# Layer 0's linear attention as two phases in one loop: a hybrid transformer on one Trainium2 core

## The reference, cut to what matters

```python
q  = x + x @ Wq.T + bq
ks = x + einsum(x, Wk) + bk        # two sets
vs = x + einsum(x, Wv) + bv        # two sets
q, ks = silu(q) + 0.5, silu(ks) + 0.5
q  = q / (norm(q) + 1e-6);  ks = ks / (norm(ks) + 1e-6)       # by head of 8 channels
states = einsum('kbhnd,kbhne->kbhde', ks * scale, vs * scale)
state  = prod(states, axis=0)      # the product of the two sets
out = q @ state                    # by head
out = (out - mean) * rsqrt(var + 1e-5) * ln_g + ln_b
out = out @ Wo.T + bo
```

## Time and profile before

| | |
|---|---|
| median of three runs | 6225.26 us (6223.73 to 6227.15) |
| the profiled execution's own time | 6223.72 us |
| its span, first to last instruction | 6221.8 us |
| PE busy in the span | 3906.2 us, 63% |
| DVE busy | 3758.3 us, 60% |
| ACT busy | 2448.4 us, 39% |
| POOL busy | 1708.2 us, 27% |
| mean granted TensorE clock | 0.795 of full speed |

### The profile page before, as it was taken

The page is one execution under the profiler, slowest core; times in us unless marked ns, Lnnn a source line. Parts: engine busy times, 40 slices in busy tenths (PEclk is TensorE's granted clock), DMA queues, the critical chain, the costliest instruction groups (busy, mean ns, idle before and its releaser), DMA issues. The chain is left out here.

```text
span 6221.8 us, 78605 instructions
## 1 busy us (share of the span) xinstructions
PE 3906.2 (63%) x21844; PEld 2459.3 (40%) x21844; DVE 3758.3 (60%) x6990; ACT 2448.4 (39%) x4474; POOL 1708.2 (27%) x1709
## 2 busy tenths in 40 slices
PE   5756648466664488724666664688855847476474
PEld 3546438222233233322222223344434636454464
DVE  4323651599974677544888886655567635566354
ACT  2334226355532277613545443233333524243242
POOL 0043014355542355422333340000001140301412
PEclk8868659688876699856778785799966779887898
DMA  2012003100001222012000000000000011100111
GB/s 82 0 55 75 1 10 91 41 1 0 0 4 54 74 82 89 22 36 79 0 1 0 0 0 2 18 1 0 0 2 2 2 45 41 39 8 2 45 42 51
DMA packets 224866, 170.50 MB, mean 27 GB/s; under 512 B 27435, under 2 KB 211602, under 8 KB 223714
## 3 DMA queue, kind: packets, MB, share of 16 engines
q1 hardware_dynamic: 204130, 125.44, 6.8%
q0 software_dynamic: 20480, 41.98, 2.3%
HBM read 92.02 MB, written 74.45 MB: 27 GB/s over the span
## 5 line engine op out<-in xcount | busy, mean ns | idle before, releaser
L1775 POOL TENSOR_TENSOR XN<-s_l_attn_a_h,LOG 128x512 f32<-128x512 f32 x512 | 642.5, 1276 | 768.6 <-DVE s_l_attn_a_h L1815 753.5
L1815 DVE TENSOR_TENSOR_SCAN s_l_attn_a_h<-s_l_attn_a_da,XN 128x512 f32<-128x512 f32 x512 | 598.5, 1211 | 142.9 <-ACT s_l_attn_a_da L1760 102.7
L1751 PE MATMUL s_l_attn_a_y_ps<-XN,c_ident 128*128 128x512 f32 x1024 | 588.7, 704 | 25.2 <-DVE s_l_attn_a_y L2027 15.4
L1760 ACT ACTIVATE s_l_attn_a_da<-s_l_attn_a_delta,s_l_attn_a_a 128x510 f32<-128x510 f32 x512 | 353.3, 690 | 526.0 <-DVE s_l_attn_a_h L1815 525.5
L483 DVE COPY s_l_ffn_ffn_xt<-s_l_ffn_ffn_turned 128x128 f32<-128x128 f32 x416 | 120.9, 292 | 711.1 <-PE s_l_ffn_ffn_turned L604 709.5
L569 POOL DMA_INDIRECT s_l_ffn_ffn_back<-slots_y,s_l_ffn_ffn_slots x320 | 302.8, 946 | 875.3 <-DMA slots_y<-PICK 566.4
L623 PE MATMUL s_l_ffn_ffn_down<-down,s_l_ffn_ffn_hid 128*128 x2944 | 421.1, 284 | 193.4 <-DVE s_l_ffn_ffn_hid L496 186.0
L623 PEld LDWEIGHTS s_l_ffn_ffn_down<-down,s_l_ffn_ffn_hid 128*128 128x128 f32 x2944 | 361.2, 192 | 233.6 <-issue 228.5
L416 ACT COPY s_l_ffn_ffn_own_w<-up 128x512 f32 (+2 forms) x416 | 305.0, 734 | 375.4 <-DVE s_l_ffn_ffn_expert_no L467 277.3
L1730 PE MATMUL s_l_attn_a_spread<-s_l_attn_a_parts,s_l_attn_a_pick 96*128 96x512 bf16 x512 | 182.2, 443 | 390.3 <-DVE XN L1806 243.2
L561 POOL DMA_INDIRECT slots_x<-XN,s_l_ffn_ffn_slots x320 | 311.5, 973 | 388.9 <-DVE s_l_ffn_ffn_slots L460 293.2
(11 more groups left out here) (631 smaller groups left out, 8651.3 us busy)
## 6 DMA issues: line engine op xcount, KB each, us to landing
XNT<-slots_x SPq DMA_DIRECT2D x32, 640.0 KB, 6.3
slots_y<-LOG SPq DMA_DIRECT2D x16, 640.0 KB, 4.3
slots_y<-PICK SPq DMA_DIRECT2D x16, 640.0 KB, 4.3
s_l_attn_b_qr<-s_l_attn_b_q_rows SPq DMA_DIRECT2D x64, 144.0 KB
s_l_attn_b_kr<-s_l_attn_b_k_rows SPq DMA_DIRECT2D x64, 144.0 KB
XNT<-slots_x SPq DMA_DIRECT2D x8, 768.0 KB, 7.0
slots_x<-PICK SPq DMA_DIRECT2D x10, 512.0 KB, 6.4
slots_x<-XN,s_l_ffn_ffn_slots POOLq DMA_INDIRECT x320, 2.2
```

What stands on the lines that cost most here:

```text
L1751: last = self.nc.tensor.matmul(self.y_ps[:, i, :], self.k.ident[:], self.hc[n % 2][:, i, :], start=(n == 0), stop=(n == NST - 1))
L1760: self.nc.scalar.activation(self.da[:, i, :, 1:], self.delta[par][:, i, :].rearrange("p (b t) -> p b t", b=BPG)[:, :, 1:], ACT.Exp, scale= ...
L1775: self.nc.gpsimd.tensor_tensor(self.hc[n % 2][:, i, :], self.h[n % 2][:, i, :], self.c_rows[n % 2], ALU.mult).then_inc(self.hc_ready, 1)
L1815: self.nc.vector.tensor_tensor_scan(self.h[n % 2][:, i, :], self.da[:, i, :, :].rearrange("p b t -> p (b t)"), self.u[n % 2][:, i, :], 0.0 ...
```

## The change

The steps of a pair are split into two phases. Phase A is everything from the copy of `xg` to the masked state; phase B is everything from the product with the state to the addition to `k.X`. A helper `over_phases` runs phase A of the first pair alone, then a loop of 7 rounds, each with phase A of the next pair and phase B of this pair mixed together, and then phase B of the last pair alone. The order within a round is written out by hand for each engine. The two batches of a pair now share one `proj` and one `proj_v`: PE's projection of a batch waits until DVE has read the one before it (`since(pe, biased, u)`). The transposed queries go into banks of `proj`, the states have a bank of their own for each `m`, and the output's projection goes into `o_ps`. The output's bias matmul now stands behind the wait for `ont_ready`. `take_stats` is removed, and `build` sets `k.stats_taken` to false behind `l0_attn_b`.

The diff, cut to its core:

```diff
-        proj = s.two_ps("proj", [P, TPB, 4 * D])
-        mid, late = s.ps("mid", [P, 2, 2, SEQ]), s.ps("late", [P, 2, 2, SEQ])
...
+        proj, proj_v = s.ps("proj", [P, TPB, 4 * D]), s.ps("proj_v", [P, TPB, 2 * D])
+        st, late = s.two_ps("st", [P, 512]), s.two_ps("late", [P, 512])
+        turned_q_ps = [proj[:, m, 0:SEQ] for m in range(2)]
+        st_ps = [b[:, 0:2 * D].rearrange("p (i d) -> p i d", i=2) for b in st]
+        o_ps = [b[:, 0:SEQ].rearrange("p (t d) -> p t d", d=D) for b in late]
+        turned_o_ps = [b[:, SEQ:2 * SEQ] for b in late]
...
+        def over_phases(engine, step):
+
+            step(0, None)
+            with engine.Fori(0, PAIRS - 1) as pair:
+                step(pair * 2 + 2, pair * 2)
+            step(None, BATCH - 2)
...
 # TensorE
+            def project(u, m):
+                pe.wait_ge(xg_ready, u + 1)
+                since(pe, biased, u)
+                for t in range(TPB):
+                    xt = xg[m][:, t * P:(t + 1) * P]
+                    nc.tensor.matmul(proj[:, t, :], xt, w["L0b_w"][:, 0:4 * D], start=True, stop=True)
+                    last = nc.tensor.matmul(proj_v[:, t, 0:D], xt, w["L0b_w"][:, 4 * D:5 * D], start=True, stop=True)
+                last.then_inc(projected, 1)
+
+            def take_from_state(u, m):
+                pe.wait_ge(done, u + 1)
+                pe.wait_ge(state_ready, u + 1)
+                pe.wait_ge(qt_ready, u + 1)
...
+            def project_out(u, m):
+                pe.wait_ge(ont_ready, u + 1)
+                nc.tensor.matmul(o_ps[m], k.ones_row[0:1, 0:P], w["L0b_bo"][:], start=True, stop=False, skip_group_check=True)
...
+            def step(a, b):
+                if a is not None:
+                    project(a, 0)
+                if b is not None:
+                    take_from_state(b, 0)
+                    take_from_state(b + 1, 1)
+                if a is not None:
+                    project(a + 1, 1)
+                if b is not None:
+                    turn_out(b, 0)
+                    turn_out(b + 1, 1)
+                    project_out(b, 0)
+                    project_out(b + 1, 1)
+                if a is not None:
+                    turn_and_add_up(a, 0)
+                    turn_and_add_up(a + 1, 1)
...
 # ScalarE
+            def step(a, b):
+                if a is not None:
+                    keep_x(a, 0)
+                    keep_x(a + 1, 1)
+                    activate(a, 0)
+                    activate(a + 1, 1)
+                if b is not None:
+                    keep_out(b, 0)
+                    keep_out(b + 1, 1)
+                if a is not None:
+                    roots(a, 0)
+                    roots(a + 1, 1)
+                    keep_qt(a, 0)
+                    keep_qt(a + 1, 1)
...
 # VectorE
+            def step(a, b):
+                if a is not None:
+                    add_bias(a, 0)
+                if b is not None:
+                    variance(b, 0)
+                    variance(b + 1, 1)
+                if a is not None:
+                    add_bias(a + 1, 1)
+                if b is not None:
+                    normalise(b, 0)
+                    normalise(b + 1, 1)
+                if a is not None:
+                    square(a, 0)
+                    square(a + 1, 1)
+                    scale(a, 0)
+                    scale(a + 1, 1)
+                if b is not None:
+                    add_out(b, 0)
+                    add_out(b + 1, 1)
+                if a is not None:
+                    mask_state(a, 0)
+                    mask_state(a + 1, 1)
...
-                take_stats(nc, dve, k, pair * (2 * TPB), 2 * TPB)
...
-            k.stats_taken = step not in ("l3_attn_a", "l2_ffn", "l3_attn_b", "l1_attn_a", "l1_attn_b", "l2_attn_a")
+            k.stats_taken = step not in ("l0_attn_b", "l3_attn_a", "l2_ffn", "l3_attn_b", "l1_attn_a", "l1_attn_b", "l2_attn_a")
```

More of the change, by code:

```diff
@@ L1006, in l0_attn_b @@
     HD = 8
-    BPG = 1
+    PAIRS = BATCH // 2
     with Scope(nc, name) as s:
@@ L1045, in _ @@
         def _(pe):
-            pe.wait_ge(w_ready, 1)
[L1047 to L1089, removed]
@@ new lines, in project @@
+            def project(u, m):
[10 more added lines that the diff above has]
+                pe.wait_ge(qt_ready, u + 1)
+                for t in range(TPB):
+                    last = nc.tensor.matmul(o_ps[m][:, t, :], qt[m][:, t * P:(t + 1) * P], state[m][:], start=True, stop=True)
+                last.then_inc(o_ready, 1)
@@ new lines, in turn_out @@
+            def turn_out(u, m):
+                pe.wait_ge(on_ready, u + 1)
+                for t in range(TPB):
+                    last = nc.tensor.transpose(turned_o_ps[m][:, t * P:(t + 1) * P], on[m][:, t, :], k.ident[:])
+                last.then_inc(turned_o, 1)
+            def project_out(u, m):
+                pe.wait_ge(ont_ready, u + 1)
+                nc.tensor.matmul(o_ps[m], k.ones_row[0:1, 0:P], w["L0b_bo"][:], start=True, stop=False, skip_group_check=True)
+                for t in range(TPB):
+                    last = nc.tensor.matmul(o_ps[m][:, t, :], ont[m][:, t * P:(t + 1) * P], w["L0b_wo"][:], start=False, stop=True,
+                                            skip_group_check=True)
+                last.then_inc(y_ready, 1)
@@ new lines, in turn_and_add_up @@
+            def turn_and_add_up(u, m):
+                pe.wait_ge(unit, u + 1)
+                for t in range(TPB):
+                    last = nc.tensor.transpose(turned_q_ps[m][:, t * P:(t + 1) * P], a[m][:, t, 0:D], k.ident[:])
+                last.then_inc(turned_q, 1)
+                for i in range(2):
+                    for t in range(TPB):
+                        last = nc.tensor.matmul(st_ps[m][:, i, :], a[m][:, t, (1 + i) * D:(2 + i) * D], z[m][:, t, (3 + i) * D:(4 + i) * D],
+                                                start=(t == 0), stop=(t == TPB - 1))
+                last.then_inc(stated, 1)
@@ L1117, in _, with add_bias @@
+            over_phases(act, step)
         @block.vector
         def _(dve):
+            def add_bias(u, m):
+                dve.wait_ge(projected, u + 1)
+                for t in range(TPB):
+                    nc.vector.tensor_tensor(z[m][:, t, 0:4 * D], proj[:, t, :], w["L0b_b"][:, 0:4 * D], ALU.add)
+                nc.vector.tensor_tensor(z[m][:, :, 4 * D:5 * D], proj_v[:, :, 0:D],
+                                        w["L0b_b"][:, 4 * D:5 * D].rearrange("p (a d) -> p a d", a=1).to_broadcast([P, TPB, D]),
+                                        ALU.add).then_inc(biased, 1)
@@ new lines, in normalise, with add_out @@
+            def normalise(u, m):
+                dve.wait_ge(rstd_ready, u + 1)
+                for t in range(TPB):
+                    last = nc.vector.tensor_scalar(on[m][:, t, :], o_ps[m][:, t, :], mv[m][:, t, 0:1], rstd[m][:, t:t + 1], ALU.subtract, ALU.mult)
+                last.then_inc(on_ready, 1)
+            def add_out(u, m):
+                dve.wait_ge(y_ready, u + 1)
+                x = k.X[:, bass.ds(u * TPB, TPB), :]
+                nc.vector.tensor_tensor(x, x, o_ps[m], ALU.add).then_inc(done, 1)
@@ L1180, in l3_attn_b @@
+            over_phases(dve, step)
 def l3_attn_b(nc, k, name):
```

126 lines of the change are left out of this document (46 added, 80 removed).

## The result

The changed kernel takes 6177.94 us (median of four runs, 6169.83 to 6182.17) against 6224.49 us (6219.08 to 6227.15): a ratio of 0.9925, 95% interval 0.9908 to 0.9942. It is 46.6 us faster; the forecast was 36.5 us, and the range (6176 to 6208) held the time, 2 us from its lower end. The profiled execution took 6169.83 us, with a span of 6168.0.

What follows compares the result with a forecast made beforehand. No engine full, a chain through all engines bounds the round; overlapping phases gives seven rounds of 21.18 us, a block 41.5 us shorter, less 5.0 us for statistics: -36.5 us from 6225.26, forecast 6188.7 us, range 6176 to 6208.

Steps and rivals of the forecast that it cites:

- What bounds the round: Old round of 27.66 us: no engine full, a chain from one engine to the next; phase B's 8.70 us can overlap.
- Steps 1 to 4: New round's first projection, first bias, wait plus second projection, second bias: 2.36, 1.62, 2.46 and 1.54 us.
- The added wait: Second projection waits for DVE's first bias because proj is shared: 2.46 us with hand-over, DVE's variances covered beside it.
- Step 5: Two normalisings on DVE, the part of phase B that stays on the path: 1.46 us.
- Step 6: Squares and scaling of both batches on DVE: 9.10 us, with PE's output work and ACT's roots beside it.
- Step 7: PE's transposes and states of the second batch, up to DVE's mask: 2.64 us at the lower clock.
- Ahead of the loop: Phase A of the first pair alone, from its first projection at 634.13 to 656.9, second projection taken as 3.3 us.
- behind it: Last masks (0.65 us) and phase B of the last pair alone (8.70 us), after the seven rounds.
- Statistics: Taken in the next layer norm: 6.68 us instead of 1.65, 5.0 more; in the new loop between 0 and 9.4.
- Sum: Block 41.5 us shorter, statistics 5.0 us more: -36.5 us, to 6188.7 us.
- Signs: Trace marks expected: clock over 0.75, three named DVE waits, PE's wait about 4 us, later sublayers unchanged in length.
- The rival in which every burst starts slow and both projections stay slow: PE at the lower clock throughout: 25.6 us a round, 6220 us; rounds of 24.6 to 26.4 us were given 7%.

Runs made afterwards that it cites:

- serial: Changed kernel with phase A and phase B of each pair run one after the other, no overlap: 6249.46 us, ratio 1.0038 to the kernel before.
- stats_in: Changed kernel with the statistics back in the loop, behind the two additions of phase B: 6180.50 us, ratio 0.9929 to the kernel before.
- again: The changed kernel timed once more with no edit: 6176.20 us, ratio 0.9921 to the kernel before.
- sq_fill: Changed kernel with squares on ACT (outputs kept first), statistics in the loop, and unused matmuls added on PE: ratio 0.9906 to the kernel before on a slower chip.
- sq_no_fill: Changed kernel with squares on ACT (outputs kept first) and statistics in the loop, no added matmuls: 6172.43 us, ratio 0.9912 to the kernel before.
- best: Changed kernel with a proj per batch, squares on ACT (outputs kept after the roots) and statistics in the loop: 6183.22 us, ratio 0.9930 to the kernel before.
- square_act: Changed kernel with the squares of a taken by ACT instead of DVE: 6177.19 us, ratio 0.9923 to the kernel before.
- two_proj: Changed kernel with a proj and proj_v for each of the two batches: 6175.46 us, ratio 0.9915 to the kernel before.
- best2: Changed kernel with a proj per batch, statistics in the loop, squares on ACT with outputs kept first: ratio 0.9922 to the kernel before on a slower chip.

## Why the prediction was right, and where its sizes were off

The forecast's way and mechanism were right, its size was 10 us short, and the range held. By its own steps:

- *What bounds the round.* Right: the chain named there is the one in the trace, and serial shows that the gain is the overlap.
- *Steps 1 to 4.* 2.36, 1.62, 2.59 and 1.53 us, where 2.36, 1.62, 2.46 and 1.54 stood. The added wait cost what was said; variances and POOL were covered.
- *Step 5*, normalising: 1.28 us, not 1.46. In the old rows POOL's wait stood between the batches; without it the four instructions overlap a little (1.36 us for all), and the squares start 0.08 us before their end.
- *Step 6:* 9.09 against 9.10.
- *Step 7* is the term that was mis-sized. From the scaled `a` (697.40) to the next projection it was 2.07 us in the round shown, and 2.64 was taken from a burst wholly at the lower clock. Here the clock rose within the burst, and its last eight matmuls took 1.54 us for 1.92. That is 0.37 of the 0.57 us. The other 0.20 is a slip of the sum: it ran to DVE's mask (699.67), and the next projection starts at 699.47. The round: 20.5 and not 21.18; over seven rounds 4.6 us.
- *Ahead of the loop* 21.7 and not 22.8 us, *behind it* 8.5 and not 9.35: 1.9 us together. Ahead, the second projection took 2.59 us from the bias before it where 3.3 stood, as it ran at the high clock (1.10 us for its first pair) after an idle time of 1.8, and the last step 2.24 for 2.64. Behind, the way from the second normalising to the last addition took 4.19 us for 5.09, with 0.69 us for the first output's bias where the old round had 1.22. For the most part this is the clock again, at its higher level where the old rows had the lower one.
- *Statistics:* 5.04 against 5.0 in the layer norm. What the forecast left open, their cost in the new loop, was nothing (stats_in), so the 5.0 us could have been kept.
- *Sum:* -36.5, less 4.6 and 1.9, is -43.0; the stretch gave -43.2. The other 3 us of the measured 46.6 lie in sublayers that weren't touched, and aren't explained. So the measured gain is 10 us above the forecast, 6.7 of it inside the stretch: the range held the time by its width.
- *Signs.* Granted clock over 0.75 in the loop: 0.76. Waits of DVE 1.5, 0.6 and 1.05 where 1.7, 0.4 and 1.1 were named. No wait for roots. PE's wait for the scaled `a` was 1.9 us a round, not about 4: the output's projections ran at the lower clock and ended late. The sublayers behind were to be unchanged in length, and were not (see `again`).

On ACT the table load of 1.28 us (689.50) was over at 690.78, and the root of the first batch started at 690.95, 0.04 us after its input was ready: no drain of the length that the Trainium skill (ScalarE: Activation LUTs, on what a table load costs) adds shows between them. In sq_fill, where the roots' input was ready before the load, they start 0.02 us after its end (765.21 and 1.28 us, then 766.51). The rival in which every burst starts slow and both projections stay slow (6220, some 31 us over the forecast) is refuted: all fourteen projections of the loop took 1.02 to 1.10 us for their first pair of matmuls.

## What to carry to other kernels

Where no engine is full and the chain goes through all of them, look at what of the next unit needs nothing of this one, and put it beside the tail; the gain can be worked out from the trace beforehand, term by term: 36.5 us here, where the stretch gave 43.2. When the chain gets shorter, read the clock of what remains on it before cutting further: 1.9 us less on DVE gave nothing while ACT's order and the clock were left as they were, 1.2 us a round with ACT's order mended and one `proj` (20.52 to 19.36 in the mean of six rounds, changed against sq_no_fill), and 1.5 us where the clock was high in both kernels (19.98 to 18.47). And before taking work out of a loop, see whether it is on the path there: these statistics were free in the loop and cost 5 us outside. Gains of 5 and 8 us inside the stretch (stats_in, best) didn't show in the medians of this 6200 us kernel.

## What the runs showed of the hardware

Five kernels without added matmuls came to nearly the same round although their DVE work differs by 2 us: 20.49 (changed), 20.48 (stats_in), 20.49 (square_act), 20.42 and still growing (two_proj), 20.46 and still growing (best). The chain isn't the same in them: in the sixth round PE waited for the scaled `a` in changed, stats_in and two_proj (1.91, 1.90 and 2.90 us), and not in square_act and best. In each the granted clock rose within the burst of states and projection, where PE had come out of a stretch of idle gaps and short matmuls, and the point of the rise was not the same: the last eight matmuls of the states took 1.49 us in the sixth round of changed and stats_in, 1.65 in square_act, 1.76 in best and 1.91 in two_proj, against 1.06 at the higher clock. That the rise comes later where the chain is shorter fits two_proj and best, round by round; that it pulls every kernel to 20.5 is not shown, and best2 and sq_no_fill (means of 19.95 and 19.36 at 0.74 and 0.77) speak against it. Other work on PE did change it: at 0.99 and 1.00 the rounds were equal to 0.01 us from the third on, at 19.98 and 18.47.
